# TensorE's order in an adaLN block with linear attention and an MoE feed-forward: the fourth transpose chunk of the next batch moved behind the fourth Q chunk

## The reference

```
h   = layernorm(x) * (1 + ca) + sa
Xn  = layernorm(h) * gamma + beta
Q, K, V = split(Xn @ W_in + b_in);  K, V = rotary(K), rotary(V)
A   = 0.5 * sum_over_tokens(K/|K| * V/|V|) + 0.5        # one row of 512 for a batch
x   = x + ga * ((A * Q) @ W_out + b_out + h)
h   = layernorm(x) * (1 + cb) + sb
x   = x + gb * (relu(h @ W_up.T) @ W_down.T + sum(softmax(top2(h @ W_gate.T))) * (h @ W_expert))
```

## Time and profile before

| what | value |
|---|---|
| time, median of 3 runs | 385.92 us (385.58 to 386.85) |
| time of the profiled execution | 386.43 us |
| span of the profiled execution | 384.6 us |
| TensorE busy | 367.0 us, 95% |
| VectorE busy | 255.4 us, 66% |
| ScalarE busy | 166.7 us, 43% |
| GpSimd busy | 113.3 us, 29% |

### The profile page before, as it was taken

How to read it: one execution, slowest core, us unless ns; L and a number is a source line. 1 busy time by engine, 2 the same in 40 slices (tenths; PEclk the granted TensorE clock), 3 DMA queues, 4 the chain that set the end, 5 groups by cost and what they waited for, 6 DMA issues and landing times.

```text
span 384.6 us, 4649 instructions
## 1 busy us (share of the span) xinstructions
PE 367.0 (95%) x1664; PEld 286.9 (75%) x1664; DVE 255.4 (66%) x515; ACT 166.7 (43%) x293; POOL 113.3 (29%) x110
## 2 busy tenths in 40 slices
PE   4997999899997999989999999999999999999996
PEld 0155888678885888868788878888788878887885
DVE  0677799869978488876887559727550855084354
ACT  1337388884427821075314681247114612541210
POOL 0114683276932528425163151910000001000000
PEclk9988899999999899999999999999999999999999
DMA  7995964050030000000000002100200110011002
GB/s 222 378 388 191 348 258 168 0 164 2 2 82 2 0 0 2 27 2 2 0 27 2 0 0 111 28 2 27 82 2 0 55 56 0 0 57 55 2 0 109
DMA packets 10951, 27.42 MB, mean 71 GB/s; under 512 B 1185, under 2 KB 1569, under 8 KB 9777
## 3 DMA queue, kind: packets, MB, share of 16 engines
q1 hardware_dynamic: 10928, 27.13, 19.8%
HBM read 22.90 MB, written 4.23 MB: 71 GB/s over the span
## 4 chain that ended last, share of the span: by engine, by line
PE 66%; DVE 12%; issue 7%; ACT 6%; DMA 4%; POOL 2%; SPq 1%; DVEq 0%; ACTq 0%; POOLq 0%
PE ps L1032 19%; PE ps L1034 19%; PE ps L1033 19%; PE ps L1039 3%; PE ps L1056 2%; DMA xs<-in_wmod 2%; DMA xs<-in_X 2%; ACT sqj L444 2%; DVE hb L657 1%; PE ps L1047 1%; ACT ps L493 1%; DVE ps L690 1%; PE ps L1159 1%; PE ps L1160 1%; ACT t_hi L495 1%
## 5 line engine op out<-in xcount | busy, mean ns | idle before, releaser
L1032 PE MATMUL ps<-w_hi,t_hi 128*128 128x512 f32 x192 | 75.7, 394 | 0.0
L1034 PE MATMUL ps<-w_hi,t_lo 128*128 128x512 f32 x192 | 75.2, 392 | 0.0
L1033 PE MATMUL ps<-w_lo,t_hi 128*128 128x512 f32 x192 | 75.2, 392 | 0.0
L1032 PE MATMUL ps<-t_hi,w_hi 128*128 128x512 f32 x128 | 51.6, 403 | 0.0
L1032 PE MATMUL ps<-w_hi,g_hi 128*128 128x512 f32 (+1 forms) x132 | 51.3, 389 | 0.3 <-DVE g_lo L743 0.3
L1034 PE MATMUL ps<-w_hi,g_lo 128*128 128x512 f32 (+1 forms) x132 | 50.6, 383 | 0.0
L1033 PE MATMUL ps<-w_lo,g_hi 128*128 128x512 f32 (+1 forms) x132 | 50.5, 383 | 0.0
L1034 PE MATMUL ps<-t_hi,w_lo 128*128 128x512 f32 x128 | 50.4, 393 | 0.0
L1033 PE MATMUL ps<-t_lo,w_hi 128*128 128x512 f32 x128 | 50.4, 393 | 0.0
L683 DVE TENSOR_TENSOR t_lo<-ps,t_hi 128x512 fp32r<-128x512 f32 x32 | 21.8, 688 | 32.9 <-ACT t_hi L495 32.6
L1032 PEld LDWEIGHTS ps<-w_hi,t_hi 128*128 128x128 f32 x192 | 36.5, 190 | 7.6
(11 more groups left out here) (130 smaller groups left out, 613.8 us busy)
## 6 DMA issues: line engine op xcount, KB each, us to landing
xs<-in_X SPq DMA_DIRECT2D x4, 1024.0 KB, 7.5
stage<-in_w SPq DMA_DIRECT2D x4, 1024.0 KB, 6.8
out<-xs SPq DMA_DIRECT2D x15, 256.0 KB, 2.0
xs<-in_wmod SPq DMA_DIRECT2D x3, 1024.0 KB, 9.8
xs<-in_wmod SPq DMA_DIRECT2D x8, 256.0 KB, 7.0
stage<-in_w SPq DMA_DIRECT2D x8, 256.0 KB, 9.6
gate_bc<-mod_rows SPq DMA_DIRECT2D x8, 256.0 KB, 6.7
gate_bc<-in_wmod SPq DMA_DIRECT2D x1, 1024.0 KB, 11.9
```

The costliest lines, as they stand in the source:

```text
L1032: mm(dst, l_hi, r_hi, start=start, stop=False)
L1033: mm(dst, l_hi, r_lo, start=False, stop=False)
L1034: return mm(dst, l_lo, r_hi, start=False, stop=stop)
```

## The change

In the four calls of `attention`, the transposes of chunk 3 leave their place directly behind those of chunk 2, ahead of the fourth Q chunk, and stand behind the fourth Q chunk, ahead of `a_sums`.

```
@@ -1119,9 +1119,8 @@
                     if c == 1:
                         transposes(b + 1, 0)
                         transposes(b + 1, 1)
-                    if c == 2:
-                        transposes(b + 1, 2)
-                        transposes(b + 1, 3)
+                    if c >= 2:
+                        transposes(b + 1, c)
                 a_sums(b)
```

## The result

The changed kernel is slower: 390.83 us (median of 4 runs, 389.62 to 391.25) against 385.75 (384.56 to 386.85), a ratio of 1.0127 with a 95% interval of 1.0089 to 1.0165. Two later series of the same kernel gave 392.1 us (6 runs, ratio 1.015, 1.0109 to 1.0192) and 390.68 (12 runs, ratio 1.0076, 1.0043 to 1.0108). This last ratio leaves out three of the 12 runs that are classed as slow because they are the longest; the median of all 12 is 1.2% above the 386.18 us of the kernel before beside them. Over all its 22 runs the median is 390.8 us, over 105 later runs of the kernel before 386.4: 4.4 us more. I had said 388.9, with a range up to 390.6. The sign was right, the size was not. Of the 1.9 us that are missing, 0.5 is in the starting point, since the median of the first three runs before (385.92) lay under that of the 105; the other 1.4 is in the change's own effect, 4.4 in place of 3.0.

What follows compares the result with a forecast made beforehand. TensorE, busy 367.0 of 384.6 us, was taken as nearly the whole question, with batch 0's path led by other engines. 1.77 - 0.4 + 0 + 1.64 = +3.0 us on the 385.92 median gave 388.9 us, range 387.1 to 390.6.

Steps and rivals of the forecast that it cites:

- The chain of batch 0: Batch 0: chunk 3's later read-out delays normalise_x, q_evac, the last g_lo and the chain through DVE to 122.88: +1.77 us.
- Batch 2: ab_col in batch 2 still ends with POOL's third addition, so q_evac and the output product stay: 0 us.
- Batch 3's wait: Gate logits behind batch 3 wait for chunk 3's t_lo and start at 225.63 instead of 223.99: +1.64 us.
- (a): It gets faster: TensorE keeps what it wins in batches 0 to 2 against batch 3's loss; -2.3, 383.6 us; 4 in 100.
- (b): Batch 0's loss is absorbed by slack between 86 and 122 us; 387.2 us; 13 in 100.
- (d): In batch 2 ab_col misses POOL's third addition and takes the next one's end; +1.25, 390.2 us; 8 in 100.
- (e): Nothing measurable, because the chunk's read-out is early enough after all; about 386 us; 2 in 100.
- the term of batch 3: Batch 3: uncovered read-out of chunk 3 delays the gate logits, straight on TensorE, no gap behind it: +1.64 us.
- rival (c): TensorE's clock falls in a new gap; in batch 3 that costs 1.6 us more, so 390.5 us; 20 in 100.
- the term of batch 1: Batch 1: normalise_x leaves ACT at 130.44, so the output product's last quarter starts at 136.42 instead of 136.83: -0.4 us.
- theory S: Batch 1's half clock costs the kernel before almost nothing, as the output product hangs on g_lo; filling its waits changes nothing.

Runs made afterwards that it cites:

- only0: The changed kernel with the move kept in batch 0 alone, the other batches as before: median 386.02 us, ratio 1.0018.
- not3: The changed kernel with the move in batches 0 to 2 and batch 3 as before: median 387.92 us, ratio 1.005.
- only12: The changed kernel with the move kept in batches 1 and 2 alone: median 386.04 us, ratio 0.9985.
- fill3: The changed kernel with six added matmuls of unused result in batch 3's gap, ahead of the gate logits: median 389.04 us, ratio 1.0079.
- exphi: The changed kernel with six of the first expert tile's twelve matmuls moved ahead of the gate logits: median 387.87 us, ratio 1.0046.
- fill1: The kernel before with nine added matmuls of unused result in batch 1's two waits: median 384.68 us, ratio 0.9964.
- fill1q: As fill1, and normalise_x of the batch after next moved on ScalarE behind the next first K/V tile's squares: median 384.94 us, ratio 0.9976.
- only3: The changed kernel with the move kept in batch 3 alone, the other batches as before: median 389.48 us, ratio 1.0075.
- qfirst: The changed kernel with normalise_x moved on ScalarE from behind the fourth chunk's read-out to behind the first K/V tile's squares: median 389.93 us, 6 runs.
- after: The changed kernel in its first series, median 390.83 us; its profiled execution took 389.62 us.
- again: The changed kernel, unchanged, in a second series: median 392.1 us, ratio 1.015; its profiled execution took 393.16 us.

## Why the prediction was wrong, point by point

**Right.** *The chain of batch 0* was read rightly: +1.77 foretold, +1.66 in the profile and +1.71 alone (only0). *Batch 2*: 0, and `ab_col` ended with POOL's third addition (180.69 against 180.66). *Batch 3's wait*: +1.64 foretold, +1.54 measured, and no later stage gave any of it back. That the fourth Q chunk would fill the wait, and that the time kept there would be lost again in front of the output product, is what the waits for `g_lo` show. Rivals (a), (b), (d) and (e) fall.

**The step that failed: the term of batch 3.** I put it at +1.64 us, the wait alone, "straight on TensorE", and left the clock's fall behind that wait out of the sum, as rival (c) with 20 in 100. The runs showed 1.5 to 1.6 us of wait and, in most executions, another 1.65 for the fall. Its price in rival (c) was right (1.6 us) and its 390.5 us was nearly the median, but I made the case without it the likeliest. How often it happens can only be estimated, from the mean clocks of the runs. In the profiles the half clock comes in stretches of 3.4 us, alone or two together, and one stretch takes 0.0044 off the mean (what begins in the last 1.4 us of a span takes less and is not counted). In the six kernels that leave neither batch 1's pair of waits nor batch 3's gap open (not3, only12, fill3, exphi, fill1, fill1q; 72 runs) the start alone makes two to four stretches, 3.0 on average. The changed kernel's 22 runs have 3.95 on average, 0.95 more. If the start is the same in all kernels, about nine in ten of them fall once more; with so few runs it can be anything from half of them to all. Where they fall, the one profile that shows it has it at 229 us, as only3 and qfirst have it in the same gap. The kernel before, over 105 runs, has 3.90, and so falls about as often, in both its profiles at 124 us. But only0, with batch 1 as before, has 3.0 on average (12 runs), no more than the start's, and two of the changed kernel's three profiles have no fall: what decides, in one and the same gap, whether the clock falls, stays open.

**A second error, which did not change the number: the term of batch 1 was right only against an execution with the half clock.** I compared one execution with a fall with a forecast without one. As most runs of the kernel before have that fall, the -0.4 us held for the medians too; that was luck, as I did not know it. Each sum of legs with and without the falls:

| | before | changed | difference |
|---|---|---|---|
| no fall | 310.84 (fill1) | 314.95 (after) | +4.1 |
| fall, each at its own place | 312.10 (before) | 316.53 (again) | +4.4 |
| my comparison: fall before, none after | 312.10 | 314.95 | +2.85 |

The measured 4.4 us between the medians is near the second line; against my +3.0 the difference is the fall in batch 3 (1.6) less 0.15 of small errors in the terms. In batch 1 the move is no gain at all against a kernel whose clock stays up: 49.32 against 48.47 us, 0.85 slower, because the read-out of Q then starts by `normalise_x`, which stands behind the late chunk. What it wins against a kernel with the fall is the half clock (1.23 us) less that 0.85, my -0.4. My theory S for fill1 had it that the half clock costs the kernel before almost nothing, since the output product hangs on `g_lo`. It does, but `g_lo` hangs on `ab_col`, and `ab_col` on the slow matmuls.

So the change removes a gap in the middle of a stage and opens one in front of the next. It gives the half clock one place less and one place more: 1.23 us saved in batch 1, 1.6 paid in batch 3, plus the waits.

The rule that I cited from the Trainium skill (TensorE: Matmul & The Clock Gate, Why this matters for your kernels), that idle gaps between bursts of matmuls bring the clock down, agreed with the trace in kind; but the gaps behind which the clock fell here, 1.41 us in batch 3 and 1.32 and 0.62 us in batch 1, are shorter than those that the page warns of, so here the traces decide. The contention rule of the Trainium skill (GPSIMD Engine Reference, Key points) held where I used it: `ab_col` took 0.88, 0.87 and 1.33 us in batches 1 to 3 of the kernel after, while POOL worked, and 0.16 us in batch 0, from 81.39, where POOL's first addition only starts at 81.51.

## What to carry to other kernels

Before moving work out of a wait, ask what its late result starts on the *other* engines: here the transposes' read-out stood in front of `normalise_x` and of Q's scaling in ACT's queue, and TensorE's saved time was spent waiting for them. When a profile shows a half clock, do not take it as fixed: estimate how many runs have it, by their mean clocks, and compare kernels with it and without it, or one execution sets the comparison. And a short gap in front of a dense stage can be dearer than its length: here 1.5 to 1.6 us of waiting cost 3.2 with the fall. A few matmuls in it kept the clock up, and real work that was ready (exphi) won the wait back as well.

## What the runs showed of the hardware that I had not expected

Nine matmuls without use made the kernel before 1.5 us faster by the medians (0.9964, 0.9941 to 0.9987), 1.2 by the legs. The clock fell behind a wait of 1.41 us that followed four tiny matmul pairs, and behind two waits of 1.32 and 0.62 us with four transposes between them (in all four profiles that have the pair), but not every time: two of the five profiles with the 1.41 us have no fall. It fell in no profile behind batch 0's four waits of 0.63 and 0.31 us between bursts of three matmuls, nor behind batch 2's 0.83 and 0.62 us, nor behind the single wait of 1.3 us that the moved transposes leave in batch 1. The spread of runs of one kernel (383 to 389 us before) is largely the clock at the start: two, three or four stretches of half clock in the first 46 us move the first of the four places from 70.5 to 74.9 us, while the legs behind it agree to 0.05 us between executions with the same falls.
